# A recommendation tower with a cubic second layer: the second layer of the last four sample tiles is done a quarter tile at a time, with the products as the stationary operand in column quarters of TensorE

## What is computed

```python
e = jnp.stack([tbl_0[ids[:, 0]], ..., tbl_31[ids[:, 31]]], axis=1)          # (1024, 32, 32)
x = e
for W in (W0, W1):                                                          # W0 (1024,128), W1 (4096,128)
    z = jnp.einsum('bhd,bmd->bhmd', e, x).reshape(b, 32 * x.shape[1], 32)
    x = jnp.einsum('bpd,pj->bjd', z, W);  res.append(x)
z = jnp.sum(jnp.concatenate(res, axis=1), axis=-1)                          # (1024, 256)
h = jnp.concatenate([z, dense_ctx], axis=1)
h = jnp.maximum(h @ W_top1 + b_top1, 0)                                     # 512
h = jnp.maximum(h @ W_top2 + b_top2, 0)                                     # 256
y = h @ W_top3                                                              # (1024, 1)
```

## Time and profile before

| | |
|---|---|
| median of 3 runs | 361.77 us (361.23 to 362.09) |
| profiled execution | 362.34 us, span of its trace 360.5 us |
| instructions | 11477 |
| PE busy | 321.7 us, 89% of the span |
| ACT busy | 242.9 us, 67% |
| DVE busy | 198.0 us, 55% |
| POOL busy | 246.0 us, 68% |
| mean granted TensorE clock | 0.976 of full |

### The profile page before, as it was taken

The page is one execution under the profiler, slowest core; times in us unless marked ns, Lnnn a source line. Parts: engine busy times, 40 slices in busy tenths (PEclk is TensorE's granted clock), DMA queues, the critical chain, the costliest instruction groups (busy, mean ns, idle before and its releaser), DMA issues.

```text
span 360.5 us, 11477 instructions
## 1 busy us (share of the span) xinstructions
PE 321.7 (89%) x4680; PEld 299.3 (83%) x4680; DVE 198.0 (55%) x702; ACT 242.9 (67%) x774; POOL 246.0 (68%) x262
## 2 busy tenths in 40 slices
PE   1999918767879989998999899989997999899997
PEld 1887817566779989998999899989987889899897
DVE  4348989676055555555654665566455545455301
ACT  1588744965558697768776876787687666767702
POOL 5777777777777777777777777777777777772000
PEclk9999976999699999999999999999999999999999
DMA  7901000000011000111001100101011010000000
GB/s 226 324 16 17 13 14 16 15 13 15 15 16 16 15 16 16 17 15 15 15 16 16 16 15 16 16 16 18 15 15 16 15 16 15 16 16 7 3 2 0
DMA packets 10772, 9.78 MB, mean 27 GB/s; under 512 B 4664, under 2 KB 8896, under 8 KB 10720
## 3 DMA queue, kind: packets, MB, share of 16 engines
q0 software_dynamic: 8192, 4.21, 7.9%
q1 hardware_dynamic: 2528, 4.84, 3.9%
HBM read 9.03 MB, written 0.00 MB: 25 GB/s over the span
## 4 chain that ended last, share of the span: by engine, by line
PE 58%; POOL 16%; ACT 9%; issue 8%; DVE 6%; DMA 2%; SPq 0%; DVEq 0%; ACTq 0%
PE WA L857 19%; POOL emb L317 16%; PE PA L812 11%; PE QB L826 6%; DVE RT L482 4%; PE PA L767 3%; PE QB L772 3%; ACT TS L324 3%; PE M L870 3%; ACT eblk L324 3%; PE T L840 2%; PE M L889 2%; PE M L880 2%; DMA TS<-in_W 1%; PE ET L799 1%
## 5 line engine op out<-in xcount | busy, mean ns | idle before, releaser
L317 POOL DMA_INDIRECT emb<-in_table,rows x256 | 245.3, 958 | 80.4 <-issue 77.4
L704 DVE COPY TS<-T 32x64 f32<-32x64 f32 x256 | 55.4, 217 | 92.4 <-PE T L840 85.4
L812 PE MATMUL PA<-eblk,zP 128*128 128x132 f32 x512 | 74.7, 291 | 2.0 <-issue 1.2
L812 PEld LDWEIGHTS PA<-eblk,zP 128*128 128x128 f32 x512 | 65.5, 198 | 9.3 <-issue 6.5
L324 ACT ACTIVATE TS<-T 32x64 f32<-32x64 f32 (+1 forms) x320 | 66.5, 208 | 7.8
L857 PE MATMUL WA<-TS,RT 128*128 128x128 f32 x512 | 61.0, 275 | 0.3 <-ACT TS L324 0.3
L324 ACT ACTIVATE TS<-PA 128x396 f32<-128x396 f32 (+1 forms) x96 | 43.4, 464 | 26.3 <-PE PA L812 25.8
L857 PEld LDWEIGHTS WA<-TS,RT 128*128 128x128 f32 x512 | 59.0, 192 | 0.6 <-ACT TS L324 0.6
L324 ACT ACTIVATE eblk<-eT 32x256 f32<-32x256 f32 x128 | 53.5, 418 | 3.1
L667 DVE TENSOR_TENSOR zP<-ET,eT 128x512 f32<-128x512 f32 x32 | 22.1, 692 | 32.7 <-ACT eT L324 32.4
L678 DVE TENSOR_TENSOR zQ<-ET,eT 128x1024 f32<-128x1024 f32 x32 | 38.9, 1215 | 0.0
(11 more groups left out here) (91 smaller groups left out, 366.7 us busy)
## 6 DMA issues: line engine op xcount, KB each, us to landing
emb<-in_table,rows POOLq DMA_INDIRECT x256, 2.4
TS<-in_W SPq DMA_DIRECT2D x8, 256.0 KB, 5.3
wt<-in_W_top SPq DMA_DIRECT2D x2, 512.0 KB, 8.6
y1w<-in_W_rows SPq DMA_DIRECT2D x1, 448.0 KB, 6.8
TS<-in_W_rows SPq DMA_DIRECT2D x1, 448.0 KB, 8.4
sym<-in_W_cols SPq DMA_DIRECT2D x1, 264.0 KB, 2.7
TS<-in_W_cols SPq DMA_DIRECT2D x1, 264.0 KB, 3.0
idc<-in_ids SPq DMA_DIRECT2D x1, 128.0 KB, 2.0
```

The source lines that it names most:

```text
L317: eng.indirect_dma_start(emb[par][:, g, :], None, table, bass.IndirectOffsetOnAxis(rows[:, k, g:g + 1], 0))\
L704: eng.tensor_copy(view(ts[32 * q:32 * q + 32, :, :], P * REST + b0, [[4 * P, 2], [P, 4], [1, 8]]), view(src, q, [[C17, 2], [4, 4], [C33, 8 ...
L812: m = eng.matmul(PA[t % 2][:, NQ * C33 * x:NQ * C33 * x + NQ * C33].rearrange("p (v c) -> p v c", c=C33), zP[u % 2][:, g, :], eblk[u % 2][ ...
```

## The change

For tiles 0 to 3 nothing is changed, but for one thing: the whole second layer of tile 3 (56 matmuls) now stands in `fill(16)`, where before it was spread over units 16 to 19. `S0` = 4 is the first tile that is done in the new way, and `WIDE` = 16 its first unit.

From tile 4 on the second layer is done for one unit at a time, one unit behind the triple products, by `narrow(v, part)`. The operands change places: the slot of `TS` with the unit's 32 samples is stationary (128 x 32), the merged weights (128 x 128) move. Each product of 32 columns stands in one quarter of TensorE's columns and of the partitions of the bank WA; the 56 matmuls go around the four quarters, so each quarter of the bank holds a partial sum. Part 0 is 48 matmuls, at the start of the next unit; part 1 is the last 8 together with 7 of the first layer (in columns 128 to 255 of WA, on quarters 2 and 3), behind `other_triples` of the next unit. The quarters are then copied to `S` (ACT the upper 64 partitions, `s_copy`; DVE the lower 64, `s_half`), and `select(v)` multiplies S by a table `sel` of four stacked 32x32 identities: it sums the quarters and turns the result to 128 x 32, in columns 256 to 319 of the same bank. ACT copies that to the unit's columns of `zf` (`n_copy`), which has two buffers now. The head keeps its matmuls. That of tile 6 moves forward, to units 29, 30 and 31. In `last_tile` unit 31 uses the bank ET in place of WA.

```diff
+        S0 = 4
+        WIDE = UNITS * S0
+        L1_AT = {4 * k + 7: k for k in range(TILES - 2)} | {ALL - 3: END - 1}
+        L2_AT = {u + 1: k for u, k in L1_AT.items()}
+        Y_AT = {u + 2: k for u, k in L1_AT.items()}
...
+            def s_copy(v):
+                n = v - WIDE
+                eng.wait_ge(s_made, n + 1)
+                wait(eng, n_made, n - 1)
+                copy(S[n % 2][64:P, :], narrow_bank(v)[64:P, 0:2 * P]).then_inc(s_kept, 1)
+            def n_copy(v):
+                k, unit = divmod(v, UNITS)
+                eng.wait_ge(n_made, v - WIDE + 1)
+                wait(eng, l1_made, k - 1)
+                copy(zf[k % 2][:, :, 32 * unit:32 * unit + 32],
+                     narrow_bank(v)[:, 2 * P:2 * P + 64].rearrange("p (c b) -> p c b", b=32)).then_inc(n_kept, 1)
...
                 part_copy(TRIOS * u)
                 part_copy(TRIOS * u + 1)
                 across_copy(u)
+                if WIDE < u < ALL - 1:
+                    s_copy(u - 1)
                 part_copy(TRIOS * u + 2)
+                if WIDE < u < ALL - 1:
+                    n_copy(u - 1)
...
+            def s_half(v):
+                n = v - WIDE
+                eng.wait_ge(s_made, n + 1)
+                wait(eng, n_made, n - 1)
+                eng.tensor_copy(S[n % 2][0:64, 0:P], narrow_bank(v)[0:64, 0:P]).then_inc(s_also, 1)
...
+            def narrow(v, part):
...
+                if part == 0:
+                    eng.wait_ge(p_kept, TRIOS * (v + 1))
+                    eng.wait_ge(q_kept, 2 * (v + 1))
...
+                    else:
+                        eng.wait_ge(n_kept, v - WIDE)
...
+                    for n in range(F + HALF):
+                        j, kt = n % NQ, KT_ORDER[n]
+                        eng.matmul(bank[32 * j:32 * j + 32, 0:P], ts[:, slot_of(kt), cols], c_slot(kt),
+                                   start=(n < NQ), stop=(j >= 2 and n >= F + HALF - NQ))
+                    return
+                for x in range(KT - F - HALF):
+                    kt, j = KT_ORDER[F + HALF + x], x % 2
+                    if x < Y1T:
+                        eng.matmul(bank[64 + 32 * j:96 + 32 * j, P:2 * P], ts[:, Y1_SLOTS[x], cols], y1w[:, x, :],
+                                   start=(x < 2), stop=(x >= Y1T - 2))
+                    m = eng.matmul(bank[32 * j:32 * j + 32, 0:P], ts[:, slot_of(kt), cols], c_slot(kt),
+                                   start=False, stop=(x >= KT - F - HALF - 2))
+                m.then_inc(s_made, 1)
+            def select(v):
...
+                for c in range(2):
+                    m = eng.matmul(narrow_bank(v)[:, 2 * P + 32 * c:2 * P + 32 * c + 32], S[n % 2][:, P * (1 - c):P * (2 - c)], sel[:, :],
+                                   start=True, stop=True)
+                m.then_inc(n_made, 1)
...
             def last_tile():
-                second(END, 0, 24)
-                result(END - 1)
-                second(END, 24, F + HALF)
-                first(END)
-                second(END, F + HALF, KT)
...
+                narrow(ALL - 2, 1)
...
+                narrow(ALL - 1, 0)
+                narrow(ALL - 1, 1)
+                select(ALL - 2)
...
+                select(ALL - 1)
+                eng.wait_ge(n_kept, ALL - WIDE)
...
             def fill(u):
+                if u > WIDE:
+                    narrow(u - 1, 0)
+                    if u == WIDE + 3:
+                        first(S0 - 1)
+                    if u in L2_AT:
+                        hidden2(L2_AT[u])
+                    return
+                n0, n1 = (0, KT) if u == WIDE else pieces(k - 1)[i:i + 2]
...
                 other_triples(u)
+                if WIDE < u < ALL - 1:
+                    narrow(u - 1, 1)
                 triples(TRIOS * u + 2)
+                if WIDE < u < ALL - 1:
+                    select(u - 1)
```

More of the change, by code:

```diff
@@ L123, in dlrm_cin_tower @@
         TH = sb("TH", [P, F, THIRD])
-        zf = sb("zf", [P, 2, P])
+        zf = [sb(f"zf{i}", [P, 2, P]) for i in range(2)]
+        sel = sb("sel", [P, 32])
+        S = [sb(f"S{i}", [P, 2 * P]) for i in range(2)]
         h1 = sb("h1", [P, N1, P])
@@ L188, in dlrm_cin_tower @@
         y1_kept = sem("y1_kept")
+        sel_made = sem("sel_made")
+        s_made = sem("s_made")
+        s_kept = sem("s_kept")
+        s_also = sem("s_also")
+        n_made = sem("n_made")
+        n_kept = sem("n_kept")
         l1_made = sem("l1_made")
@@ L204, in dlrm_cin_tower, with ts_free, narrow_bank @@
         CB = KT // 4
+        S0 = 4
[3 more added lines that the diff above has]
+        Y_AT = {u + 2: k for u, k in L1_AT.items()}
+        def ts_free(eng, k):
+            if k - 2 < S0:
+                wait(eng, y2_made, k - 1)
+                wait(eng, y1_made, k - 1)
+            else:
+                eng.wait_ge(s_made, UNITS * (k - 1 - S0))
+        def narrow_bank(v):
+            return ET if v == ALL - 1 else WA
         def trio(r):
@@ L439, in _ @@
                         e_copy(u)
-                    if k >= 2 and i == 0:
-                        hidden1(k - 2)
+                    if u in L2_AT:
+                        hidden1(L2_AT[u])
                     if 0 < len(mine) < 5:
@@ L450, in _ @@
                         rest_copies(u - 1, others.pop(0))
[L451 to L455, removed]
+                if u in Y_AT:
+                    y_copy(Y_AT[u])
+                if k >= 1 and i == 3 and k < S0:
                     y2_copy(k - 1)
+                if u == WIDE:
+                    y2_copy(S0 - 1)
+                if k >= 1 and i == 3 and k <= S0:
                     y1_copy(k - 1)
@@ L748, in _ @@
                     rest_sums()
-            for j in range(by_vector(ALL - 1)):
-                rest_copies(ALL - 1, j)
+                if u == 2 * UNITS:
+                    eng.wait_ge(const_s, 2)
+                    for j in range(NQ):
+                        eng.tensor_copy(sel[32 * j:32 * j + 32, :], ident[32 * j:32 * j + 32, 32 * j:32 * j + 32]).then_inc(sel_made, 1)
+                    for i in range(2):
+                        eng.memset(S[i][0:64, P:2 * P], 0.0).then_inc(sel_made, 1)
+                if WIDE < u:
+                    if u == ALL - 1:
+                        for j in range(by_vector(u)):
+                            rest_copies(u, j)
+                    s_half(u - 1)
+            s_half(ALL - 1)
             eng.wait_ge(tower_loaded, 16 * 5)
@@ L871, in first @@
                 m.then_inc(y1_made, 1)
-            def hidden1(k):
-                eng.wait_ge(y1_kept, k + 1)
-                eng.wait_ge(y2_kept, k + 1)
+            def narrow(v, part):
+                k, unit = divmod(v, UNITS)
+                bank, cols = narrow_bank(v), slice(32 * unit, 32 * unit + 32)
+                ts = TS[k % 2]
+                if part == 0:
+                    eng.wait_ge(p_kept, TRIOS * (v + 1))
+                    eng.wait_ge(q_kept, 2 * (v + 1))
+                    if v == ALL - 1:
+                        eng.wait_ge(z_made, NZ * ALL)
+                    elif v == WIDE:
+                        eng.wait_ge(y2_kept, S0)
+                    else:
+                        eng.wait_ge(n_kept, v - WIDE)
+                else:
+                    eng.wait_ge(t3_kept, kept_before(v + 1))
+                    eng.wait_ge(t3_also, also_before(v + 1))
+                if part == 0:
+                    for n in range(F + HALF):
[11 more added lines that the diff above has]
+                m.then_inc(s_made, 1)
@@ L879, in hidden1 @@
                     for c in range(2):
-                        eng.matmul(M[:, a, :], wt1[:, c, cols], zf[:, c, :], start=(c == 0), stop=False)
+                        eng.matmul(M[:, a, :], wt1[:, c, cols], zf[k % 2][:, c, :], start=(c == 0), stop=False)
                     m = eng.matmul(M[:, a, :], wt1d[:, cols], dT[:, P * k:P * k + P], start=False, stop=True)
@@ L936, in fill @@
                 k, i = divmod(u, UNITS)
[L937 to L940, removed]
+                if u in Y_AT:
+                    result(Y_AT[u])
                 news = list(FIRST_UNIT[u]) if u < len(FIRST_UNIT) else []
@@ L955, in fill @@
                     second(k - 1, n0, n1)
-                if n1 == KT and n0 < KT or k == 1 and i == 3:
+                if i == 3:
                     first(k - 1)
-                if k >= 2 and i == 0:
-                    hidden2(k - 2)
+                if u in L2_AT:
+                    hidden2(L2_AT[u])
             for u in range(ALL):
```

59 lines of the change are left out of this document (32 added, 27 removed).

## The result

The change makes the kernel slower: 384.56 us in the median of 4 runs (381.84 to 386.53) against 361.93 in 4 of the kernel before, a ratio of 1.062 (95% interval 1.058 to 1.066), 22.6 us. The prediction had the sign and not the size: it forecast 369.2, in a range up to 375. The profiled execution took 381.84 us with a span of 378.8, 18.3 longer than that of before.

The account below looks back on a forecast made before the run. PE was taken as the bound; from unit 16 at 191.58, 18.1 + 110.0 + 27.0 + 7.8 + 13.5 = 176.4 us gave a span of 368.0, 7.4 more than before, so a median of 369.2. Range: 361.5 to 375.

Parts of the forecast that it names:

- What bounds the kernel: Whole kernel: PE is the bound nearly all the way, with at most 3.7 us of gather waits to win.
- Unit 16: 12.51 + 1.79 + 3.77 = 18.07: Unit 16 on PE: whole second layer of tile 3, `hidden2` and every unit's common work, 18.07 us in all.
- what is queued behind the new copies: ACT and DVE: S copy holds the last PA copy and next eT; `s_half` (0.28 us) holds T3 copies, then products.
- No clock effect: PE's granted clock is full, 2.4 GHz, from slice 12 of 40, so none plays where the change acts.
- The price of the narrow form: Narrow matmuls on PE: 0.0279 us an instruction, 2.68 for part 0 and 0.84 for part 1.
- The rival on the faster side: Narrow instructions at line 826's 0.0155 us, gathers then decide: time 349.6 us; 12% for any pace on that side.
- four by 0.10, eight by 0.26: Table reading for line 840's quarter instructions, used towards its pace of one four each 0.11 us.
- The plain unit: Units 17 to 30 on PE: 7.86 us each, `select` 0.35 of it; plain units 8.1 to 8.2 apart.
- The loop through WA: Part 0 waits for `n_copy` of the unit before: 0.3 us in seven units, 2.1 in all.
- The rival of the loop as a bound: Copies or matmuls in one bank make each unit wait 0.8 to 1 us: 376 us; chance 10%.
- The end: Unit 31 takes 7.8 us, and the rest from part 1 of unit 30 to the end 13.5.

Follow-up runs that it names:

- split_call: The changed kernel with the second layer of tile 3 in unit 16 called in three pieces (32, 16 and 8 products): 376.1 us, ratio 1.037.
- part1_early: split_call with part 1 and `select` moved forward, on ACT `s_copy` ahead of `across_copy` and `n_copy` ahead of the last `part_copy`: 375.7 us, ratio 1.037.
- no_sums: split_call without `select` and the copy of its result to `zf` from tile 4 on, so `y1` and `y2` are missing there: 365.95 us, ratio 1.010.

## Why the prediction was right and wrong

*What bounds the kernel: right.* PE's work decides, the 3.7 us of waits were hardly anything to fill, and they went to 0.5. The tail shrank by 8.9 us and the time grew.

*"Unit 16: 12.51 + 1.79 + 3.77 = 18.07": this step failed.* It has no term for a wait, and 25.50 us were measured. The work was priced exactly, as split_call shows with 18.07, but the waits that move with it were not. `second` puts its waits ahead of its first product. With 9 products only those of PA are awaited; with all 56 also those of QB and T3 (lines 844 to 852), and the order of ACT puts the copies out of T3 of unit 15 some 5.7 us behind the transposes. The prediction listed what is queued behind the new copies on ACT and DVE; the waits of `second` itself, moved and made larger, it put at nothing. 5.83 us of idle and 1.61 of low clock in the profiled execution: 7.4 of the 10.8 us by which the span missed its 368.0.

*No clock effect: wrong through the same step.* It was read off a profile in which PE has no such idle time from slice 12 on. Behind 5.8 us of idle PE runs 3.25 us at a granted 0.50; in split_call, without the idle time, the same stretch has 1.00. The other three executions of the change list a mean clock of 0.955 to 0.960 against 0.968 here and spans of 381.5 to 383.7; whether the low clock lies at the same place there is not shown, since only one was traced.

*The price of the narrow form: right.* 64 instructions from 218.14 to 219.91 are 0.0277 each in this trace, taken as 0.0279 from line 840; line 826 did not apply. The rival on the faster side falls with that. The four quarters overlap: 4 x 0.0277 is the 0.111 of one instruction at full width. (The prediction's "four by 0.10, eight by 0.26" of the earlier trace rows mixes busy time and length of the stretch; eight by 0.16 of busy time is what the row says. The price is not touched by it.)

*The plain unit: 8.16 forecast, 8.34 measured,* 3.5 us over units 17 to 30 (140.5 between the transposes, 137.0 in the sum). `select` is 0.44, where I took 0.35 between two bounds: the upper one was the price, 0.11 an instruction although only 32 columns move behind a load of 128. The Trainium skill ("TensorE: Matmul & The Clock Gate", LDWEIGHTS) puts a load at its columns over 1.2, in ns, which makes an estimate of 0.43 for the four; the trace agrees. I had set that aside because the instructions of line 826, with loads of 32 columns, take 15.5 ns each where it gives 27. A rule that does not fit one size may hold for the size in question. The other 0.09 is 0.07 in the last triples ahead of `select` (0.62 for 0.55) and 0.05 of wait ahead of part 0, less a little elsewhere; part 0 and the first triples behind it, 4.30, were priced right with 4.34. Of the 3.5 us, `select` makes 1.3 and those triples 0.9; another 1.0 is `result`, 0.64 behind a wait of 0.91 (1.08 in unit 17), where 0.45 and 0.9 were taken.

*The loop through WA: the size right, the cause too narrow.* 0.3 of wait ahead of part 0 were forecast, and 0.35 are there. The places were wrong: forecast were units 18, 20, 22, 24, 26, 28 and 30, but `hidden1` covers the wait of the unit behind it, so the trace has it in units 18, 19, 22, 23, 26 and 27. That six times 0.35 make the 2.1 of seven times 0.3 is luck. And part1_early and no_sums show that without the wait for the zf copy there is one for the last copy out of PA instead. The rival of the loop as a bound falls. The Trainium skill ("TensorEngine Tiling (Array Packing)", PSUM Bottleneck) says that after a fourfold speedup the copies out of PSUM may become the bound, a "may" that the prediction dropped. This case shows no such bound: ACT stays at 66%, and what remains is that wait for copies in order, 0.35 us in six units.

*The end: 21.3 forecast for unit 31 and the last tile, 21.85 measured* (from 356.95, where the transposes end in pace), and from the first matmul of the second hidden layer to the end 4.8 as before.

Together: 7.4 + 3.5 + 0.55, less 0.66 since unit 16 started earlier, are the 10.8 us of the span. split_call, without the 7.4, is still 6.2 above the forecast span: the 3.5 and 0.55 again, and 2.1 since unit 16 started later. So the wait is the largest miss and not the only one. The rest of the median's 15.4 above the forecast lies in the runs: the profiled execution is the fastest of the four, 2.7 under the median, it has 3.0 us around its span where that of before has 1.8, and that of before was 0.6 above its median. Where the slower three lose their time is open.

Not settled: whether an order exists that brings both ACT's last copy out of PA and the zf copy forward, and what narrow and dense products in separate banks, which cut the loop, would give. No run here tries either.

## What to carry to other kernels

When a call is moved or made larger, list its waits again, not only its work: a wait at the head of a long call holds everything behind it for what only its last part needs. Before shortening the tail of a kernel, count how much idle time the bounding engine has ahead of it, and where it lies: work done sooner is only free in those gaps, and here they were 3.6 us (8.5 with the waits of `result` moved), against 3.6 us of overhead in each of four tiles.

## What the runs showed of the hardware

An fp32 instruction at full width with a load of 128 columns takes 0.11 us whether 128 columns move behind it (0.1117) or 32 (`select`: 0.44 for four), while four 128-column products on the four column quarters together take the 0.11 us of one at full width. After 5.8 us without matmuls TensorE ran its next 15 instructions at 0.217 us each, granted 0.50, then 38 in 4 us, granted 1.00.
